# One unit of the patch tokenizer in another order: value quarters, scores, squares and means, keys and projection, and GpSimd's patch sums

## The reference

```
x = features.reshape(b, c, h, 4, w, 4)
reduce_feats = x.mean((3, 5))                        # one mean pixel per patch
q = layernorm(reduce_feats) @ Wq.T                   # 8 heads of 8 channels
k, v = layernorm(the 16 pixels of the patch) @ Wkv.T
attn = softmax(q * scale . k)                        # over the 16 pixels
out = reduce_feats + (attn . v) @ proj_w.T + proj_b
```

## Time and profile before

| | |
|---|---|
| median of three runs | 922.05 us (919.56 to 923.01) |
| profiled execution, its own time | 924.28 us |
| its span from first to last instruction | 922.5 us, granted clock 0.981 |
| TensorE busy | 859.5 us, 93% |
| VectorE busy | 744.4 us, 81% |
| ScalarE busy | 495.5 us, 54% |
| GpSimd busy | 524.2 us, 57% |
| instructions | 22430 |

### The profile page before, as it was taken

One profiled execution on the slowest core, in us unless ns is written; L12 is line 12 of the kernel. 1 busy time (PEld: TensorE's weight loads), 2 busy tenths in 40 slices (PEclk: granted clock), 3 DMA queues, 4 the chain that ended last, 5 costly groups with the idle time before them and its releaser, 6 DMA issues.

```text
span 922.5 us, 22430 instructions
## 1 busy us (share of the span) xinstructions
PE 859.5 (93%) x8584; PEld 351.3 (38%) x8584; DVE 744.4 (81%) x1271; ACT 495.5 (54%) x767; POOL 524.2 (57%) x387
## 2 busy tenths in 40 slices
PE   5799999999999999999999998676999999999996
PEld 1234334333343343343433433232444444444442
DVE  6788888888888888888888888997677878778784
ACT  3655455454554554554545522258666666666652
POOL 2789899999999898999998954000211102111100
PEclk9999999999999999999999999979999999999997
DMA  9568979979888789798798853000000000000000
GB/s 361 170 193 244 273 222 252 281 219 252 264 238 263 240 244 269 229 253 279 222 254 257 244 125 92 0 1 0 0 12 12 13 24 12 23 12 12 24 12 36
DMA packets 49053, 141.51 MB, mean 153 GB/s; under 512 B 5440, under 2 KB 5440, under 8 KB 40768
## 3 DMA queue, kind: packets, MB, share of 16 engines
q1 hardware_dynamic: 48960, 140.17, 51.3%
HBM read 68.85 MB, written 4.19 MB: 79 GB/s over the span
## 4 chain that ended last, share of the span: by engine, by line
PE 37%; POOL 25%; issue 14%; DMA 11%; SPq 8%; DVE 4%; ACT 1%; POOLq 1%; DVEq 0%; ACTq 0%
DMA sb_arena<-x 10%; SPq L532 7%; POOL sb_prodv L589 5%; POOL sb_rows L490 5%; PE ring L1131 5%; PE ring L1101 4%; PE bank_ms L1143 3%; POOL sb_wgt L582 3%; POOL sb_score L571 3%; POOL sb_wgt L577 3%; POOL sb_rows L492 3%; POOL sb_rows L485 2%; PE qp L1086 2%; PE bank_ms L1138 2%; PE ring L900 2%
## 5 line engine op out<-in xcount | busy, mean ns | idle before, releaser
L900 PE MATMUL ring<-sb_arena,sb_wqkv 64*64 64x512 f32 x2048 | 255.1, 601 | 4.5 <-DVE sb_prodv L1303 2.9
L1272 DVE TENSOR_TENSOR sb_prodk<-ring,sb_qbuf 128x1024 f32<-128x1024 f32 x128 | 153.3, 1219 | 18.6 <-PE ring L900 15.4
L637 POOL TENSOR_TENSOR sb_parts_q<-sb_arena,sb_const 128x512 fp32r<-128x512 f32 x15 | 15.6, 1039 | 267.4 <-DVE sb_arena L1545 267.4
L485 POOL TENSOR_TENSOR sb_rows<-sb_arena 128x2048 f32<-128x2048 f32 x31 | 141.7, 4571 | 29.1 <-DMA sb_arena<-x 28.9
L1303 DVE TENSOR_TENSOR sb_prodv<-ring,sb_wbc 128x1024 f32<-128x1024 f32 x128 | 150.9, 1201 | 2.1 <-issue 2.1
L681 ACT ACTIVATE sb_xsq<-sb_arena 128x2048 f32<-128x2048 f32 x64 | 118.4, 1896 | 3.7 <-DMA sb_arena<-x 3.7
L939 PEld LDWEIGHTS qp<-sb_prodv,sb_tok_w 64*64 64x64 f32 x3072 | 89.0, 133 | 69.8 <-POOL sb_prodv L589 34.4
L939 PE MATMUL qp<-sb_prodv,sb_tok_w 64*64 64x128 f32 x3072 | 101.8, 271 | 10.2 <-POOL sb_prodv L589 9.6
L900 PEld LDWEIGHTS ring<-sb_arena,sb_wqkv 64*64 64x64 f32 x2048 | 65.7, 132 | 118.0 <-issue 93.9
L589 POOL TENSOR_TENSOR sb_prodv<-sb_prodv 128x256 f32<-128x256 f32 x128 | 93.0, 738 | 11.2 <-DVE sb_prodv L1303 11.2
L652 ACT ACTIVATE sb_means<-sb_sum 128x256 f32<-128x256 f32 x32 | 13.3, 416 | 117.8 <-POOL sb_sum L495 115.8
(11 more groups left out here) (244 smaller groups left out, 1487.2 us busy)
## 6 DMA issues: line engine op xcount, KB each, us to landing
sb_arena<-x SPq DMA_DIRECT2D x64, 1024.0 KB, 8.8
sb_wbc<-sb_wgt SPq DMA_DIRECT2D x256, 256.0 KB, 4.9
out<-sb_arena SPq DMA_DIRECT2D x16, 256.0 KB, 2.0
sb_rest_w<-rest_w SPq DMA_DIRECT2D x1, 918.5 KB, 22.4
sb_const<-const SPq DMA_DIRECT2D x1, 264.5 KB, 3.3
sb_tok_w<-tok_w SPq DMA_DIRECT2D x1, 260.5 KB, 2.9
sb_const<-const SPq DMA_DIRECT2D x1, 256.0 KB, 23.5
```

The source lines that it names most:

```text
L485: eng.tensor_tensor(rows[:, :, :, :], pix[:, :, 0:8], pix[:, :, 8:16], ALU.add).then_inc(sum8_ready, 1)
L900: mm = pe.matmul(ring[slot][C * half:C * half + C, i, :], image_block(w, i), x[C * i:C * i + C, m, half, c], start=True, stop=True)
L1272: dve.tensor_tensor(by_pixel(prodk[:, c]), by_pixel(ring[c % 2][:, :, :]), q[:, :, None, :].to_broadcast([P, 2, N_PIX, G32]), ALU.mult).th ...
```

## The change

On TensorE the keys of quarter 1 move behind p0 and those of quarter 2 behind p1. The first values quarter moves ahead of the scores. The means move from the end of the step to directly behind the squares, so that the query and only one values quarter stand at the end. On VectorE the first value product moves ahead of the scaling of the scores; the sum and inverse of the weights move behind the third value product, and the two variances ahead of the fourth, with the pixels' first. On ScalarE `pixel_mean` moves ahead of the query's three steps. On GpSimd the first patch sums of a unit are done at the end of the step before, behind the last two `add_pixels`, which come into their own unit's step. No instruction is added or removed, and no wait is changed.

```diff
@@ gpsimd
             norm_scores(0)
+            patch_sums_first(pool, 2, 2)
             def step(n, m):
-                prev = not isinstance(n, int) or n >= 1
...
-                if nxt2:
-                    patch_sums_first(pool, n + 2, (m + 2) % NF)
-                if prev:
-                    add_pixels(n - 1, 2)
-                    add_pixels(n - 1, 3)
+                nxt3 = not isinstance(n, int) or n + 3 < UNITS
                 if nxt2:
                     patch_sums_rest(pool, n + 2)
...
                 if nxt:
                     norm_scores(n + 1)
+                add_pixels(n, 2)
+                add_pixels(n, 3)
+                if nxt3:
+                    patch_sums_first(pool, n + 3, (m + 3) % NF)
             pipeline(pool, step, UNITS)
-            add_pixels(UNITS - 1, 2)
-            add_pixels(UNITS - 1, 3)
@@ scalar
                 if nxt2:
+                    pixel_mean(n + 2)
                     q_square(n + 2)
                     q_rstd(n + 2)
                     query(n + 2, m)
-                    pixel_mean(n + 2)
@@ tensor
                     keys(n + 1, m1, 0)
-                    keys(n + 1, m1, 1)
                 if prev:
                     project(n - 1, 0)
                 if nxt:
-                    keys(n + 1, m1, 2)
+                    keys(n + 1, m1, 1)
                 if prev:
                     project(n - 1, 1)
                 if nxt:
+                    keys(n + 1, m1, 2)
                     keys(n + 1, m1, 3)
                 if prev:
                     project(n - 1, 2)
+                values(n, m, 0)
                 if nxt:
                     scores(n + 1)
-                values(n, m, 0)
                 values(n, m, 1)
+                values(n, m, 2)
                 if nxt2:
                     pixel_squares(n + 2, m2)
+                    pixel_means(n + 2, m2)
                     query(n + 2, m2)
...
-                values(n, m, 2)
                 values(n, m, 3)
-                if nxt2:
-                    pixel_means(n + 2, m2)
@@ vector
+                value_products(n, m, 0)
                 if nxt:
                     score_scale(n + 1)
                     score_max(n + 1)
-                value_products(n, m, 0)
                 value_products(n, m, 1)
-                if nxt:
-                    score_sum(n + 1)
-                if nxt2:
-                    query_var(n + 2)
-                if nxt:
-                    score_inverse(n + 1)
...
                 value_products(n, m, 2)
+                if nxt:
+                    score_sum(n + 1)
+                    score_inverse(n + 1)
+                if nxt2:
+                    pixel_var(n + 2)
+                    query_var(n + 2)
+                value_products(n, m, 3)
                 if nxt2:
                     query_scaled(n + 2)
-                value_products(n, m, 3)
-                if nxt2:
-                    pixel_var(n + 2)
```

## The result

The changed kernel takes 929.11 us (median of four runs, 928.56 to 929.20) against 920.95 us for the kernel before, timed beside it (four runs, 919.56 to 923.01). The ratio is 1.0086, with a 95% interval of 1.0063 to 1.0108: slower by 0.9%. The profiled execution took 928.56 us, its span 926.8.

A forecast was written before the change was run, and what follows sets the result against it. TensorE was taken to set the pace: 16.12 us of work plus a 0.90 us wait makes 17.02 a unit against 16.91, 3.3 us over 29 periods, plus 0.5 at the start: 3.8, so 926 us, range 917 to 935.

The forecast's parts named there:

- The new wait before p0: TensorE, projection's first part: waits for query_scaled, path 2.66 us less 1.76 of cover, 0.90 us a unit.
- its upper bound: Wait before p0 of 1.17 us, adding 0.12 for a matmul shape change and 0.15 for VectorE occupied; rival, 12 in 100.
- The work of 16.12 us without waits: TensorE's work for one unit without any wait, 16.12 us, taken as unchanged in the new period.
- the saving of a change of matmul shape: TensorE, squares directly ahead of means: 0.12 us a unit saved, giving 913; counted within the vp3 rival of 13 in 100.
- v0 ahead of the scores takes away their wait: TensorE before the scores: v0 lengthens the cover for kp3 from 0.87 to 1.84 us, so the 0.66 us wait goes.
- GpSimd's wait is gone: Adds 2 and 3 ahead of the patch sum: p2's wait goes, GpSimd's 15.6 us a unit fits; cost taken as nothing.
- The start: First unit costs about 0.5 us more (within 0 and 2), its vp0 ahead of the scaling and weights issued late.
- k1 behind p0 costs and gives nothing: TensorE, keys alternating with projection: same number of changes, keys covered, k2 3.56 us after k0's end; cost nothing.
- Weights landing late: Rival: weights for VectorE's vp0 land over 8.3 us after issue, delaying scores by 0.7 us; 936 to 946, 11 in 100.
- p0 waits for vp3 only: Rival: the fourth value product alone releases p0, wait 0.58 us, period 16.70, 916.5 us; 13 in 100.
- the lower bound of 0.58: Least wait before p0, in us, set by vp3 ending 2.34 after q against 1.76 of cover, however fast the query's path.
- The clock: Rival: waits in each unit lower TensorE's clock; one unit in ten at half speed adds 40 us; 2 in 100.

The follow-up runs named there:

- e2: Changed kernel with the means last again on TensorE (squares, query, v3, means), ScalarE and VectorE ordered to match: 899.78 us, ratio 0.9771 to the kernel before.
- e3: Changed kernel with query ahead of the means on TensorE, ScalarE and VectorE ordered to match: 920.62 us, ratio 0.9996 to the kernel before.
- e8: Changed kernel with the query moved behind v3 on TensorE and query_var behind the fourth value product on VectorE: 988.64 us, ratio 1.0722 to the kernel before.
- e5: Changed kernel with the waits before p0 reordered and the one for weights_scaled dropped: 924.08 us, ratio 1.0029 to the kernel before.
- e1: Kernel before with only GpSimd's new order (adds 2 and 3 ahead of the next unit's first patch sum): 917.63 us, ratio 0.9965.
- e6: e2 with GpSimd's old order (first patch sum ahead of adds 2 and 3): 931.56 us, ratio 1.0112 to the kernel before.
- e4: Changed kernel with keys 0 and 1 both ahead of p0 again, k2 and k3 each one place later: 927.54 us, ratio 1.0069 to the kernel before.
- e7: e2 with keys 0 and 1 both ahead of the projection again: 913.01 us, ratio 0.9907 to the kernel before.

## Why the prediction was right, point by point, and where its sizes were off

The cause and its place were right; the size of the loss was not. The forecast was 3.8 us more than before, and the scores of unit 31 start 7.0 us later (8.2 us by the medians). That 926 stands as near to 929 as it does is partly luck: the range was wide enough, and two errors in the unit's sum pulled in opposite directions. The median before that the forecast started from, 922.05 us, is also 1.1 us above the one timed beside the changed kernel.

*The new wait before p0* is the mechanism that the prediction named, in its place and with its releaser, and e2 shows that it turns a gain into the loss: with the wait gone the kernel is 29 us faster. e3 and e8 move it by the cover that stands behind the query. Its size was off: 1.16 us against 0.90. `query_scaled` started 0.13 later than its own path allows, since the fourth product held VectorE for 1.14 us; the prediction had left this to its upper bound. TensorE saw the release after 0.26 us rather than 0.05, which is 0.21 more. And `pixel_var` in front of `query_var` cost nothing by the time of the exponential (1.67 as worked out without it), which is 0.08 less: 0.13 + 0.21 - 0.08 = 0.26. That 0.08 was a slip in the sum: 0.77 - 0.70 + 0.69 - 0.09 is 0.67, not 0.74, and the trace has `query_var` at 0.68. Put right, the prediction's own links give a wait of 0.83, a period of 16.95 and about 924 us, further from the result. e5 takes back 0.11 of the release by the list of waits alone.

*The work of 16.12 us without waits* became 17.13 - 1.16 = 15.97. That is 0.15 less: the squares take 1.74 us with the means directly behind, 0.12 less than ahead of the query. This is the saving of a change of matmul shape that the prediction put with a rival. So the two errors partly cancel: 0.26 - 0.15 = 0.11 us a unit. Over all 29 intervals the period is (555.15 - 57.36) / 29 = 17.17 us against 17.02, which is 29 x 0.15 = 4.2 us. Of this 3.2 us are the 0.11 in each unit, 0.6 the long last period, which was not foreseen ("the end of the tokenizer is as before"), and 0.4 is spread over the rest, with three periods of 17.2 among them. Less the 1.0 us by which the start was misjudged, 3.2 us remain, and they are the difference between the forecast 3.8 and the 7.0 of the traces.

*What the change gave and what it took.* Before, a unit waited for 0.79 us on average; that is gone and worth 29 x 0.79 = 22.9 us, and the cheaper work another 29 x 0.15 = 4.4 us. The new wait takes 29 x 1.16 = 33.6 us. The balance is a loss of 6.4 us. With the 0.6 and the 0.4 above, and 0.5 less at the start, that is the 7.0 of the traces within rounding.

*v0 ahead of the scores takes away their wait*: right; e1, which lacks it, keeps that wait and e2, which has it, has none. *GpSimd's wait is gone*: right, and its price in a quick unit was measured by e6.

*The start*: 0.5 us lost was forecast; the scores of unit 2 start 0.49 us earlier. The first vp0 did wait for its weights, as said, and for 1.31 us, yet the period from unit 1 to unit 2 is 57.36 - 40.23 = 17.13 us, no longer than the later ones, while in the kernel before it was 17.70 (57.85 - 40.15):

```profile
41.48 1.23 DVE L1300 TENSOR_TENSOR sb_prodv<-ring,sb_wbc 128x1024 f32<-128x1024 f32 x1 [1.31 <-DMA sb_wbc<-sb_wgt]
```

*k1 behind p0 costs and gives nothing*: in the changed kernel it costs 1.6 us, if anything (e4), but once the means are last it is worth 13.2 us (e7). The prediction looked at the keys' own waits in the new order and not at what the old order would do there.

*The rivals.* Weights landing late: after the start no product of the steady units waits for transfers. p0 waits for vp3 only: no, but it is the next release, and e3 puts it at 0.68 us, between the lower bound of 0.58 and the wait taken. The clock: not in this kernel, where it reads 1.00 to 560 us with a wait of 1.16. But the argument for it was misread: the 1.8 us of the earlier trace rows was a wait of weight loads, while the matmuls before were still under way. The longest wait of the matmuls themselves between 60 and 540 us was 1.0 us. Gaps of 2.0 us (2.18 by starts) in every unit do take the clock down in most units (e8). By the Trainium skill's page TensorE: Matmul & The Clock Gate (A second HAM failure mode: psum-queue depth-cycling), frequent idling between groups of matmuls made the clock of one measured kernel oscillate between its two levels. The periods of 18.1 and 19.8 us in e8 agree with such an oscillation.

## What to carry to other kernels

A long piece of work that nothing waits for is not idle stuff in an order: ask what it covers. When two pieces swap, list the paths that start before them and end behind them on other engines, and add up the time that is left for each; here 5.44 us of cover became 1.76 for a path of 2.92. And try each move by itself and in the best company: GpSimd's order and the alternating keys look nearly worthless in a slow unit and are worth 32 and 13 us in a fast one.

## What the runs showed of the hardware

- With a wait of about 2.18 us on TensorE in each unit of 18 us (e8), 18 of 29 periods were 1.69 us longer than the others, at a granted clock of 0.91 over the unit where it was read, and behind the wait a keys quarter took 1.94 instead of 1.07 us. With a wait of 1.16 us in each unit of 17 us the granted clock read 1.00 throughout.
- TensorE started 0.06 us after a long product that it waited for (e3), but 0.26 us after the short `query_scaled`, of which 0.11 went when one wait was dropped and two reordered (e5).
- Squares directly ahead of means, with operands of one shape, take 1.74 us, ahead of a query 1.86.
